# The end of a two-layer Perceiver block on one core: the last groups of the second attention ordered by hand, the residual added by the matmul engine, already turned tokens quantised, stores issued from two engines

## The chip, the cores and the metric

The kernel runs on one core of one Trainium2 chip. The metric is the device time of one execution in microseconds (us). The core has a matmul engine (TensorE, PE in the rows; its weight loads are listed apart as PEld), VectorE (DVE), ScalarE (ACT), GpSimd (POOL) and SyncE (SP), which issues transfers. The engines run their own instruction lists in order and meet only at semaphores. Matmul results land in eight banks of PSUM, each 128 partitions by 512 float32 columns; everything else is in SBUF.

## What is computed

Six residual layers on `x` (4 batches of 128 tokens, 128 channels), each fed with the layer norm of `x`: a strided cross attention over 2048 context rows, a state space layer, a ternary SwiGLU, a gated cross attention, then a self attention with a relative position bias, and an MLP with quantised activations. The change touches the last two:

```
x = x + L1_attn(layernorm(x))        # 16 heads of 8 channels, softmax, out @ w_proj.T + b_proj
x = x + L1_ffn(layernorm(x))

def qlinear(x, W, b):                # L1_ffn is qlinear, gelu, qlinear
    scale = max((max(x) - min(x)) / 255, 1e-8)      # over ALL tokens and channels
    zp    = clip(round(-min(x) / scale) - 128, -128, 127)
    xq    = clip(round(x / scale) + zp, -128, 127)
    return ((xq - zp) @ wq.T) * (scale * w_scale) + b
```

The minimum and maximum run over the whole tensor, so no activation of the MLP can be quantised before the last batch has been normalised, and again not before the last hidden value is there. Rounding is done by adding and taking off `ROUND` = 12582912.

## The kernel before, in words

Each batch `b` is one tile of 128 tokens. `attention(ph)` exists once on PE, DVE and ACT and is run for both attentions (`ph` 0 and 1). In step `t` (0 to 25) the engines work on group `t` of the 16 groups (four heads of one batch each; batch `t // 4`): scores on PE (lines 1242 to 1245), on DVE the bias and row maxima (806), exponentials on ACT (498). Two steps later PE turns the group's probabilities (1264) and DVE copies them out (823). What closes a batch is tied to `t` by a table of numbers on line 63; `due(t, stage)` gives the batch whose stage falls in step `t`:

```
LAG = 2
INVERSE, INVERSE_T, VALUES, SCALE, PROJECT, ADD, RSTD, NORM, TURN = 6, 7, 8, 9, 10, 11, 11, 12, 13
```

The stages of one batch are: reciprocal of the row sums on DVE (850), turned by PE (1281) and copied out (856); the 16 products with the values on PE ("heads", 1293) into bank 5, copied to `o_T` by ACT (511); the inverse sums spread over the channels by PE (1298) into bank 7; their product `attn_T` on DVE (832); the projection on PE into bank 5 (1313); the residual plus bias `xb` added on DVE (838); mean and variance (731, 732); reciprocal deviation by two ACT instructions (430, 431); the normalised tile `xn` (736), and its extremes (784, 785). PE issues the heads of a batch only when the batch before has been added, since both use bank 5 (1289, 1290). For the last two batches the steps 16 to 25 hold little else.

Then the MLP. `extremes(i)` on PE turns the per-partition extremes (1547); DVE folds them to one column (869), puts them on a diagonal (870), PE spreads this to all partitions with a matrix of ones (1550); `range_of_all`, `affine_step` and `affine_bounds` on DVE make scale, its inverse and the clip bounds (873 to 893). DVE scales and rounds `xn` (1087), clips (1091) and takes off `ROUND` into bfloat16 (1095), in two halves; PE turns the four tiles (1556), ACT copies them to `xq_T` (699), and PE makes four hidden chunks (1561), ACT the gelu (703), DVE the extremes of each (1098, 1099). The second quantisation goes the same way, without turning: ACT rounds chunks 0 to 2 (707), DVE rounds chunk 3 (1104), clips all four (1113) and takes off `ROUND` (1121), one clip ahead; PE accumulates four batches over the chunks in the order 0, 3, 1, 2. DVE adds the residual (1127) and SP stores each batch (349), four stores on one queue.

Of the kernel before, what the change touches and what calls it, by code (L numbers as in the profile page):

```python
# [15 lines left out]
ALU = mybir.AluOpType  # L16
ACT = mybir.ActivationFunctionType
F32 = mybir.dt.float32
BF16 = mybir.dt.bfloat16
# [51 lines left out]

BY_PE = tuple(range(3, NS, 2))
# [24 lines left out]
def two_layers(nc, early, cols, late, rows, ctx_T, taps, ctx, out):  # L97
    st = ExitStack()
    with st:
# [164 lines left out]
        ext_diag = sb("ext_diag", [2 * IC, 2, 2 * IC])  # L264
        rng = sb("rng", [P, 2, 2])
        zs = sb("zs", [P, 2, 8])
        t1 = turn("mlp", [NB, D])
        t2 = turn("mlp", [NB, D])
# [17 lines left out]

        def turned_xn(n, b):
# [13 lines left out]
        def turned_xq8(half):  # L301
            return bank[6 + half][:, 0:P].bitcast(BF16)

# [7 lines left out]
            fin ext ext_ps ext_diag rng z_inv z_out xq8 xq8T xq8T_sb hid_ps hid_sb h_round h_q down8""".split()  # L311
# [12 lines left out]
        def _(sp_):  # L324
# [95 lines left out]
        def _(act):  # L420
# [54 lines left out]

            def self_keys(b):
# [6 lines left out]
            def attention(ph):  # L483
                for t in range(NG * (NB - 1) + TURN + 1):
# [21 lines left out]
                    if due(t, VALUES) is not None:  # L506
                        v = ph * NB + due(t, VALUES)
                        act.wait_ge(S["pv"], v + 1)
                        if v >= 1:
                            act.wait_ge(S["attn"], v)  # L510
                        done(act.activation(o_T[:, :], bank[5][:, 0:P], ACT.Copy), "o_sb")
# [25 lines left out]
            done(act.activation(ident_b[:, :], ident, ACT.Copy), "consts")  # L537

# [167 lines left out]
            for c in range(IC - 1):  # L706
                done(act.activation(h_r1[:, c, :], h_T[:, c, :], ACT.Identity, scale=zs[:, 1, 1:2], bias=round_col[:, :]),
                     "h_round")


        @block.vector
        def _(dve):
# [68 lines left out]

            def token_extremes(b):
# [4 lines left out]
            def attention(ph):  # L787
                i_out = 1 if ph == 0 else 5
                for t in range(NG * (NB - 1) + TURN + 1):
# [28 lines left out]
                    if 0 <= t - LAG < 4 * NB:  # L818
                        w = ph * 16 + t - LAG
                        dve.wait_ge(S["probs_T_ps"], w + 1)  # L820
                        if w // NG >= 2:
                            dve.wait_ge(S["pv"], w // NG - 1)
                        done(dve.tensor_copy(probs_T[:, w % (2 * NG)].rearrange("p h k -> p (h k)"),  # L823
                                             bank[3 + w % 2][:, :]), "probs_T_sb")
                    if due(t, SCALE) is not None:

                        v = ph * NB + due(t, SCALE)
                        dve.wait_ge(S["o_sb"], v + 1)
                        dve.wait_ge(S["spread_ps"], v + 1)
                        if v >= 2:  # L830
                            dve.wait_ge(S["proj"], v - 1)
                        done(dve.tensor_tensor(attn_T[:, v % 2, :], o_T[:, :], bank[7][:, P:2 * P], ALU.mult), "attn")
# [12 lines left out]
                    if due(t, INVERSE) is not None:  # L845
                        v = ph * NB + due(t, INVERSE)
                        dve.wait_ge(S["probs"], 4 * v + 4)
                        if v >= 2:
                            dve.wait_ge(S["invT_ps"], v - 1)
                        done(dve.reciprocal(inv_sum[:, v % 2, :], row_sum[:, v % 2, :]), "inv_sum")  # L850
                    if due(t, INVERSE_T) is not None:
                        v = ph * NB + due(t, INVERSE_T)
                        dve.wait_ge(S["invT_ps"], v + 1)
                        if v >= 1:
                            dve.wait_ge(S["spread_ps"], v)
                        done(dve.tensor_copy(inv_T[:, :], bank[7][0:NH, 0:P]), "invT_sb")
# [27 lines left out]
            def affine_bounds(i, w):  # L884
# [3 lines left out]
                at = mark(dve.tensor_scalar(z[:, 7:8], rng[:, i, 1:2], z[:, 1:2], ROUND, ALU.mult, ALU.add))  # L888
# [7 lines left out]
            link(dve.memset(round_col[:, :], ROUND))  # L896
# [757 lines left out]
```

## Time and profile before

| | |
|---|---|
| median of three runs | 275.21 us (273.03 to 277.95) |
| the profiled execution | 274.26 us, span of its records 272.5 us |
| busy over the span | PE 78%, DVE 72%, ACT 60%, POOL 27% |
| granted TensorE clock, mean | 0.906 of 2.4 GHz |
| first instruction of the part touched (copy of the last but one group) | 240.13 us |
| end of the last output store's landing | 272.5 us |

In the rows, a time is the start in us from the span's start, then the duration; `L823` is line 823; `out<-in` are the tiles; in brackets stands the engine's idle time before and who ended it. Tiles that are parts of one large buffer are all called `region`. The 32 us from 240 to the end are where all edits lie.

### The profile page before, as it was taken

The numbers are of one execution on the slowest core, as the hardware profiler recorded it, in microseconds if no ns is written. First come the engines' busy times: TensorE is split into PE (matmuls) and PEld (weight loads), VectorE is DVE, ScalarE is ACT, GpSimd is POOL, SyncE is SP. The second block draws the span as 40 slices with busy tenths as digits, with TensorE's granted clock in tenths as the row PEclk, the third lists the DMA queues.
The fourth block names the chain that finished last, engine by engine and source line by source line (L and its number), as shares of the span: only waits on it lengthen the run. The fifth ranks groups of instructions, "written<-read, shape, count | busy, mean of one in ns | idle before, by whom it ended". The sixth has DMA issues, their size and how long they took to land.

```text
span 272.5 us, 4968 instructions
## 1 busy us (share of the span) xinstructions
PE 211.6 (78%) x1632; PEld 150.0 (55%) x1634; DVE 197.4 (72%) x571; ACT 163.4 (60%) x541; POOL 74.5 (27%) x73
## 2 busy tenths in 40 slices
PE   7797897888996598889908777999987799972313
PEld 4676785777663343444504545877866789851102
DVE  5467668842398599999697665697667599985675
ACT  3685857616882788888077555134536699842520
POOL 6012100099035577878970010000010000001000
PEclk9999999999979799999975799999999799995555
DMA  6999800000005885000000032000000000000001
GB/s 230 432 384 412 357 7 2 1 2 2 0 0 62 93 93 61 2 0 1 0 0 0 4 101 53 0 2 0 2 0 2 0 2 4 1 2 1 0 0 39
DMA packets 6745, 16.06 MB, mean 59 GB/s; under 512 B 320, under 2 KB 5056, under 8 KB 5696
## 3 DMA queue, kind: packets, MB, share of 16 engines
q1 hardware_dynamic: 6720, 15.75, 20.0%
q8 instruction: 13, 0.21, 0.3%
q14 instruction: 12, 0.10, 0.1%
HBM read 13.39 MB, written 2.35 MB: 58 GB/s over the span
## 4 chain that ended last, share of the span: by engine, by line
PE 39%; DVE 27%; ACT 16%; issue 10%; POOL 5%; DMA 1%; DVEq 0%; another core or an unknown queue 0%; ACTq 0%; POOLq 0%
PE bank L1134 33%; POOL region L411 5%; ACT probs L498 4%; DVE region L958 3%; ACT region L600 3%; PE bank L1526 3%; DVE region L806 2%; DVE region L823 2%; ACT region L568 2%; PE bank L1264 2%; DVE region L775 1%; ACT k_groups L446 1%; DVE xn L736 1%; DMA early_sb<-early 1%; DVE stats L731 1%
## 5 line engine op out<-in xcount | busy, mean ns | idle before, releaser
L411 POOL TENSOR_TENSOR region<-region 128x512 f32<-128x512 f32 x32 | 40.3, 1271 | 13.3 <-DVE region L958 8.9
L958 DVE TENSOR_TENSOR_SCAN region<-region,bank 128x512 f32<-128x512 f32 x32 | 38.1, 1210 | 4.8 <-issue 2.0
L1134 PE MATMUL bank<-k_groups,region 128*128 128x128 f32 x256 | 36.1, 287 | 4.1 <-ACT k_groups L446 2.9
L1134 PEld LDWEIGHTS bank<-k_groups,region 128*128 128x128 f32 x256 | 32.2, 198 | 7.0 <-ACT k_groups L446 3.7
L1134 PE MATMUL bank<-region,early_sb 128*128 128x512 f32 x64 | 32.8, 612 | 1.2 <-POOL region L411 1.1
L380 POOL TENSOR_TENSOR xb<-x,rows_sb 128x512 f32<-128x512 f32 x3 | 3.8, 1265 | 102.6 <-DVE x L838 43.3
L498 ACT ACTIVATE probs<-bank,neg_max 128x128 f32<-128x128 f32 x64 | 22.7, 366 | 12.0 <-DVE neg_max L801 11.9
L498 ACT ACTIVATE probs<-region,neg_max 128x128 f32<-128x128 f32 x64 | 24.9, 389 | 5.4 <-DVE neg_max L806 5.2
L430 ACT ACTIVATE lnv<-mv,eps_col 128x1 f32<-128x1 f32 x24 | 7.0, 292 | 32.8 <-DVE mv L732 32.6
L1134 PE MATMUL bank<-ctx_T_sb,region 128*32 128x128 f32 (+1 forms) x288 | 25.0, 312 | 1.9 <-DVE v_heads L743 1.6
L823 DVE COPY region<-bank 128x512 f32<-128x512 f32 x32 | 21.8, 682 | 3.8 <-PE bank L1264 3.8
L1264 PE MATMUL bank<-early_sb,probs 128*128 128x128 f32 x128 | 20.4, 283 | 2.1 <-ACT probs L498 1.5
L600 ACT ACTIVATE region<-region,a_neg 128x508 f32<-128x508 f32 x32 | 21.3, 709 | 0.0
L806 DVE CUSTOM_DVE_ANT_0 region<-bank,region 128x128 f32<-128x128 f32 x64 | 14.5, 282 | 5.4 <-PE bank L1134 5.4
L801 DVE TENSOR_REDUCE neg_max<-bank 128x4 f32<-128x512 f32 x16 | 11.0, 687 | 9.0 <-PE bank L1134 9.0
L1264 PEld LDWEIGHTS bank<-early_sb,probs 128*128 128x128 f32 x128 | 14.8, 144 | 4.2 <-ACT probs L498 2.1
L1134 PEld LDWEIGHTS bank<-region,ctx_sb 128*128 128x128 f32 x128 | 15.4, 192 | 2.9 <-issue 2.9
L1065 DVE COPY region<-bank 128x512 f32<-128x512 f32 x16 | 10.9, 686 | 8.1 <-PE bank L1526 8.1
L686 ACT ACTIVATE region<-bank,shift 128x512 f32<-128x512 f32 x16 | 10.8, 689 | 8.2 <-DVE shift L1042 8.2
L1134 PE MATMUL bank<-region,ctx_sb 128*128 128x128 f32 x128 | 15.6, 275 | 0.0
L1134 PEld LDWEIGHTS bank<-region,early_sb 128*128 128x128 f32 x64 | 11.1, 196 | 7.4 <-POOL region L411 5.0
L1134 PEld LDWEIGHTS bank<-ctx_T_sb,region 128*32 128x32 f32 (+1 forms) x288 | 11.4, 118 | 4.8 <-DVE v_heads L743 1.8
(205 smaller groups left out, 444.6 us busy)
## 6 DMA issues: line engine op xcount, KB each, us to landing
ctx_sb<-ctx SPq DMA_DIRECT2D x4, 1024.0 KB, 25.1
ctx_T_sb<-ctx_T SPq DMA_DIRECT2D x3, 1024.0 KB, 10.1
late_sb<-late SPq DMA_DIRECT2D x1, 2416.0 KB, 19.3
bias_scratch<-bias_vec SPq DMA_DIRECT2D x1, 2040.0 KB, 24.7
ctx_T_sb<-ctx_T SPq DMA_DIRECT2D x2, 512.0 KB, 5.7
region<-bias_scratch SPq DMA_DIRECT2D x1, 1024.0 KB, 5.6
early_sb<-early SPq DMA_DIRECT2D x1, 512.0 KB, 3.6
region<-taps SPq DMA_DIRECT2D x1, 512.0 KB, 20.0
```

The lines of the kernel that those rows point to most:

```text
L411: done(pool.tensor_tensor(read[:, k % 3, :], state[:, k % 3, :], c_sb[:, n % 2, :], ALU.mult), "read")
L498: ins = act.activation(probs[:, w % 4, j, :], src[:, j, :], ACT.Exp, bias=neg_max[:, w % 4, j:j + 1], scale=1.0 if ph == 0 else -1.0, accu ...
L600: done(act.activation(dst, src, ACT.Exp, scale=a_neg[:, hf, n:n + 1]), "decay")
L686: done(act.activation(p2[:, b % 2, g, :], bank[g][:, :], ACT.Exp, bias=shift[:, b:b + 1], accum_out=part_sum[:, b, g:g + 1]), "p2")
L801: done(dve.tensor_reduce(neg_max[:, w % 4, :], src, AX, ALU.max, negate=True), "neg_max")
L806: ins = dve.tensor_tensor_reduce(neg_biased[:, t % 3, j, :], src[:, j, :], rel_bias[:, HG * g + j, :], -1.0, HIGHEST, ALU.add, ALU.min, ne ...
L823: done(dve.tensor_copy(probs_T[:, w % (2 * NG)].rearrange("p h k -> p (h k)"), bank[3 + w % 2][:, :]), "probs_T_sb")
L958: done(dve.tensor_tensor_scan(state[:, k % 3, :], decay[:, k % NDA, :], bank[3 + k % 3][:, :], 0.0, ALU.mult, ALU.add), "state")
L1065: done(dve.tensor_copy(p2_T[:, w % 4].rearrange("p c q -> p (c q)"), bank[4 + w % 2][:, :]), "p2T_sb")
L1134: return pe.matmul(dst, lhsT, rhs, start=start, stop=stop)
L1264: ins = pe.transpose(bank[3 + w % 2][:, j * P:j * P + P], probs[:, w % 4, j, :], ident)
L1526: ins = pe.transpose(bank[4 + w % 2][:, c * P:c * P + P], p2[:, b % 2, g, c * P:c * P + P], ident)
```

## The change

On all three engines the loop of `attention(1)` now ends after step 15, when all groups have been started (`STEPS`), and the rest is written out by hand. In it the last group's turn stands ahead of the spreading of batch 2, the heads of batch 3 wait only for `o_T` of batch 2 and no longer for batch 2's residual, the inverse sums of batch 3 use bank 2, and batches 2 and 3 are projected into banks 0 and 1 on top of a product of the identity and `xb`, which adds the residual in PE. DVE takes moments and `xn` straight from those banks; ACT copies them to `x5` later. PE turns the four `xn` tiles in float32 into bank 6 before the range is known; DVE rounds from that bank, 512 columns at once, and writes `xq_T` itself. The diagonal is replaced by a constant diagonal holding 1/255, with the extremes as broadcast weights. ACT takes `ROUND` off chunk 3. The stores of batches 1 and 3 are issued by ACT.

```diff
+STEPS = NG * (NB - 1) + TURN + 1, 4 * NB
 # sync
-            for b in range(NB):
+            for b in (0, 2):
                 sp_.wait_ge(S["x_ready"], 5 * NB + b + 1)
 # scalar
             attention(1)
+            heads_out(2 * NB - 2)
+            heads_out(2 * NB - 1)
+            rsqrt_var(5, 2)
+            rsqrt_var(5, 3)
             act.preload_act_table_set("gelu_and_others")
-            for b in range(2):
-                act.wait_ge(S["xq8T"], b + 1)
-                done(act.activation(xq_T[:, 2 * b * P:2 * (b + 1) * P], turned_xq8(b), ACT.Copy), "xq8T_sb")
+            for b in (2, 3):
+                act.wait_ge(S["xn"], 5 * NB + b + 1)
+                done(act.activation(X[5][:, b, :], late_proj(b), ACT.Copy), "x_ready")
...
+            act.wait_ge(S["h_clip"], 1)
+            done(act.activation(h_q[:, IC - 1, :], h_r2[:, IC - 1, :], ACT.Identity, bias=neg_round[:, :]), "h_q_last")
+            for b in (1, 3):
+                act.wait_ge(S["x_ready"], 5 * NB + b + 1)
+                act.dma_start(out[b], X[6][:, b, :]).then_inc(S["stored"], 16)
 # vector
-                link(dve.tensor_reduce(ext_row[:, i:i + 1], bank[7][0:2 * IC, 384:512], AX, ALU.max))
-                done(dve.tensor_scalar(ext_diag[:, i, :], ident[0:2 * IC, 0:2 * IC], ext_row[:, i:i + 1], None,
-                                       ALU.mult), "ext_diag")
+                done(dve.tensor_reduce(ext_row[:, i:i + 1], bank[7][0:2 * IC, 384:512], AX, ALU.max), "ext_row")
...
-                link(dve.tensor_scalar(z[:, 6:7], rng[:, i, 0:1], rng[:, i, 1:2], INV255, ALU.add, ALU.mult))
-                link(dve.tensor_scalar(z[:, 0:1], z[:, 6:7], 1e-8, None, ALU.max))
+                link(dve.tensor_scalar(z[:, 0:1], rng[:, i, 0:1], rng[:, i, 1:2], 1e-8, ALU.add, ALU.max))
...
-                link(dve.tensor_scalar(z[:, 2:3], z[:, 7:8], ROUND, ROUND + 255.0, ALU.max, ALU.min))
-                link(dve.tensor_scalar(z[:, 3:4], z[:, 2:3], -1.0, 2.0 * ROUND, ALU.mult, ALU.add))
-                link(dve.tensor_scalar(z[:, 4:5], z[:, 3:4], 255.0, None, ALU.add))
+                link(dve.tensor_scalar(z[:, 2:3], z[:, 7:8], ROUND, ROUND, ALU.add, ALU.max))
+                link(dve.tensor_scalar(z[:, 6:7], z[:, 2:3], ROUND + 255.0, -1.0, ALU.min, ALU.mult))
+                mark(dve.tensor_scalar(z[:, 3:4], z[:, 6:7], 2.0 * ROUND, None, ALU.add))
+                link(dve.tensor_scalar(z[:, 4:5], z[:, 6:7], 2.0 * ROUND, 255.0, ALU.add, ALU.add))
...
+            turned_probs(8 * NB - 2)
+            inverse(2 * NB - 1)
+            normed(5, 1)
+            turned_probs(8 * NB - 1)
+            scaled(2 * NB - 2)
+            inverse_turned(2 * NB - 1)
+            token_extremes(1)
+            scaled(2 * NB - 1)
+            late_moments(2)
+            late_moments(3)
+            late_normed(2)
+            token_extremes(2)
+            late_normed(3)
+            token_extremes(3)
...
+            dve.wait_ge(S["xnT_all"], 1)
+            rounded_at = mark(dve.tensor_scalar(t1, bank[6][:, :], zs[:, 0, 1:2], ROUND, ALU.mult, ALU.add))
             affine_bounds(0, 3)
             after(rounded_at)
+            link(dve.tensor_scalar(t2, t1, zs[:, 0, 3:4], zs[:, 0, 4:5], ALU.max, ALU.min))
+            done(dve.tensor_scalar(xq_T[:, :], t2, -ROUND, None, ALU.add), "xq8")
...
+            first_at = clip(0)
+            clip(last)
+            after(first_at)
+            quantised(0)
+            for c in (1, 2):
+                after(clip(c))
+                quantised(c)
 # tensor
+            def late_project(b):
+                v = NB + b
+                pe.wait_ge(S["xb_ready"], 3)
+                pe.wait_ge(S["neg_max"], 8 * NB)
+                mm(late_proj(b), ident, xb[:, b, :], True, False)
+                pe.wait_ge(S["attn"], v + 1)
+                done(mm(late_proj(b), attn_T[:, v % 2, :], L("w_projT"), False, True), "proj")
...
-            for i, c in enumerate((0, IC - 1, 1, 2)):
+            for i, c in enumerate((0, 1, IC - 1, 2)):
```

The first place is PE from the last three probability turns to the first turned extremes; here before (`inv_T` is the inverse sums, `v_heads` the values, so its row is the heads of one batch, first of batch 2, then of batch 3):

```order
L1264 MATMUL bank3<-early_sb,probs 128x128 x4
L1134 MATMUL bank5<-region,v_heads 32x128 x16
L1134 MATMUL bank7<-inv_T,cols_sb 128x128
L1264 MATMUL bank4<-early_sb,probs 128x128 x4
L1134 MATMUL bank5<-late_sb,attn_T 128x128
L1281 MATMUL bank7<-early_sb,inv_sum 16x128
L1134 MATMUL bank5<-region,v_heads 32x128 x16
L1134 MATMUL bank7<-inv_T,cols_sb 128x128
L1134 MATMUL bank5<-late_sb,attn_T 128x128
L1547 MATMUL bank7<-early_sb,ext 8x128
```

The same place on PE in the changed kernel:

```order
L1183 MATMUL bank5<-region,v_heads 32x128 x16
L1285 MATMUL bank4<-early_sb,probs 128x128 x4
L1183 MATMUL bank7<-inv_T,cols_sb 128x128
L1300 MATMUL bank2<-early_sb,inv_sum 16x128
L1183 MATMUL bank5<-region,v_heads 32x128 x16
L1183 MATMUL bank2<-inv_T,cols_sb 128x128
L1183 MATMUL bank0<-xb,early_sb 128x128
L1183 MATMUL bank0<-late_sb,attn_T 128x128
L1183 MATMUL bank1<-xb,early_sb 128x128
L1183 MATMUL bank1<-late_sb,attn_T 128x128
L1620 MATMUL bank6<-early_sb,xn 128x128 x4
L1626 MATMUL bank7<-early_sb,ext 8x128
```

Both projections have moved behind both heads, and four turns of `xn` stand ahead of the extremes.

The second place is DVE from the first quantisation's rounding to the first gelu extreme; before:

```order
L1087 TENSOR_SCALAR region<-xn,zs 128x512
L888 TENSOR_SCALAR zs<-rng,zs 128x1
L889 TENSOR_TENSOR zs<-zs,w_scale 128x1
L891 TENSOR_SCALAR zs<-zs 128x1
L892 TENSOR_SCALAR zs<-zs 128x1
L893 TENSOR_SCALAR zs<-zs 128x1
L1091 TENSOR_SCALAR region<-region,zs 128x256 x2
L1095 TENSOR_SCALAR xq<-region 128x256 x2
```

And DVE at that place in the changed kernel:

```order
L1137 TENSOR_SCALAR region<-bank6,zs 128x512
L911 TENSOR_SCALAR zs<-rng,zs 128x1
L912 TENSOR_TENSOR zs<-zs,w_scale 128x1
L914 TENSOR_SCALAR zs<-zs 128x1
L915 TENSOR_SCALAR zs<-zs 128x1
L916 TENSOR_SCALAR zs<-zs 128x1
L917 TENSOR_SCALAR zs<-zs 128x1
L1140 TENSOR_SCALAR region<-region,zs 128x512
L1141 TENSOR_SCALAR xq_T<-region 128x512
```

The bounds have one instruction more, the rounding reads a bank, and the last row writes the operand of the hidden matmul; PE's turns and ACT's copies that stood behind it are gone.

## Rows read from the trace of the kernel before

**Rows 1.** The page, part 4: shares of the chain that ended last.
```profile
PE 39%; DVE 27%; ACT 16%; issue 10%; POOL 5%; DMA 1%; DVEq 0%; another core or an unknown queue 0%; ACTq 0%; POOLq 0%
```
**Rows 2.** Windows: length, busy PE, PEld, DVE, ACT, POOL; clock, DMA share, GB/s.
```profile
243.00:245.00 2.00, 1.63 (x37) 1.13 (x34) 1.29 (x5) 0.71 (x3) 0.00 (x0) 1.00 0.04 8
245.00:246.00 1.00, 0.39 (x3) 0.25 (x2) 0.67 (x3) 0.07 (x1) 0.00 (x0) 0.52 0.00 0
262.00:270.00 8.00, 2.84 (x18) 1.96 (x18) 6.36 (x23) 2.22 (x3) 0.00 (x0) 0.50 0.00 1
```
**Rows 3.** Timeline, end of the second attention: start, us, engine, instruction, idle before.
```profile
236.66 1.06 PE L1134 MATMUL bank<-k_groups,region 128*128 128x128 f32 x8
...
240.64 0.48 PE L1134 MATMUL bank<-inv_T,cols_sb 16*128 16x128 f32 x2
...
241.06 0.66 PE L1264 MATMUL bank<-early_sb,probs 128*128 128x128 f32 x4
...
241.75 0.69 DVE L823 COPY region<-bank 128x512 f32<-128x512 f32 x1
242.36 0.28 DVE L832 TENSOR_TENSOR attn_T<-o_T,bank 128x128 f32<-128x128 f32 x1
...
242.69 0.49 PE L1134 MATMUL bank<-late_sb,attn_T 128*128 128x128 f32 x2 [0.98 <-DVE attn_T L832]
...
243.65 1.08 PE L1134 MATMUL bank<-region,v_heads 128*32 128x128 f32 x32 [0.37 <-DVE x L838]
...
245.76 0.80 PE L1134 MATMUL bank<-late_sb,attn_T 128*128 128x128 f32 x2 [0.61 <-DVE attn_T L832]
...
246.92 0.29 DVE L731 BATCH_NORM_STATS2 stats<-x 128x6 f32<-128x128 f32 x1
...
248.02 0.35 DVE L736 TENSOR_SCALAR xn<-x,mv,rstd 128x128 f32<-128x128 f32 x1 [0.60 <-ACT rstd L431]
...
248.94 0.38 PE L1547 MATMUL bank<-early_sb,ext 128*8 128x128 f32 x1 [2.39 <-DVE ext L785]
```
**Rows 4.** Timeline, range and first quantisation.
```profile
249.74 0.22 DVE L870 TENSOR_SCALAR ext_diag<-early_sb,ext_row 8x8 f32<-8x8 f32 x1
250.01 0.59 PE L1134 MATMUL bank<-ext_diag,ones 8*128 8x8 f32 x2 [0.69 <-DVE ext_diag L870]
...
251.08 0.15 DVE L880 TENSOR_SCALAR zs<-zs 128x1 f32<-128x1 f32 x1
251.27 0.16 DVE L881 RECIPROCAL zs<-zs 128x1 f32<-128x1 f32 x1
251.47 0.48 DVE L1087 TENSOR_SCALAR region<-xn,zs 128x512 f32<-128x512 f32 x1
...
252.68 0.74 DVE L1091 TENSOR_SCALAR region<-region,zs 128x256 f32<-128x256 f32 x2
...
254.81 0.13 PEld L1134 LDWEIGHTS bank<-xq_T,wq_w1T 128*128 128x128 bf16 x2 [0.80 <-ACT xq_T L699]
```
**Rows 5.** DVE reading banks, by tile, from 190 us: ns min/median/max, starts.
```profile
L778 DVE TENSOR_SCALAR region<-bank,cols_sb x16: 339/343/351, 202.9 to 223.7; 128x128 f32<-128x128 f32 x16
L823 DVE COPY region<-bank x16: 669/685/692, 209.5 to 241.7; 128x512 f32<-128x512 f32 x16
```
**Rows 6.** Groups by form, 240 to 272.5 us: busy us, mean ns, idle before.
```profile
L1113 DVE TENSOR_SCALAR region<-region,zs 128x512 f32<-128x512 f32 x4 | 2.1, 543 | 0.0
...
L1121 DVE TENSOR_SCALAR region<-region 128x512 bf16<-128x512 f32 x4 | 1.6, 420 | 0.0
```
**Rows 7.** Timeline, second quantisation and output.
```profile
264.90 1.00 DVE L1113 TENSOR_SCALAR region<-region,zs 128x512 f32<-128x512 f32 x2
...
268.73 1.12 DVE L1127 SCALAR_TENSOR_TENSOR x<-bank,zs,xb 128x128 f32<-128x128 f32 x4 [0.57 <-PE bank L1134]
269.11 1.77 SPq L349 DMA_DIRECT2D out<-x  x4
```
**Rows 8.** Transfers by line: count, KB each, median us from issue to landing.
```profile
out<-x SPq DMA_DIRECT2D x4, 64.0 KB, 1.6
```

More of the change, by code:

```diff
@@ L474, in gates, with heads_out @@
                                     ACT.Silu), "gate_sb")
+            def heads_out(v):
+                act.wait_ge(S["pv"], v + 1)
+                if v >= 1:
+                    act.wait_ge(S["attn"], v)
+                done(act.activation(o_T[:, :], bank[5][:, 0:P], ACT.Copy), "o_sb")
             def self_keys(b):
@@ L483, in attention @@
             def attention(ph):
-                for t in range(NG * (NB - 1) + TURN + 1):
+                for t in range(STEPS[ph]):
                     if ph == 0 and t % NG == 3 and t // NG + 1 < NB:
@@ L506, in attention @@
                     if due(t, VALUES) is not None:
[L507 to L511, printed above, removed]
+                        heads_out(ph * NB + due(t, VALUES))
                     if due(t, RSTD) is not None:
@@ L537, in _ @@
             done(act.activation(ident_b[:, :], ident, ACT.Copy), "consts")
+            done(act.activation(ident_255[:, :], ident[0:2 * IC, 0:2 * IC], ACT.Copy, scale=INV255), "consts")
             a_rates = a_neg[:, :, :].rearrange("p a n -> p (a n)")
@@ L788, in attention @@
                 i_out = 1 if ph == 0 else 5
-                for t in range(NG * (NB - 1) + TURN + 1):
+                for t in range(STEPS[ph]):
                     if t < 4 * NB:
@@ L818, in attention @@
                     if 0 <= t - LAG < 4 * NB:
[L819 to L824, printed above, removed]
-                    if due(t, SCALE) is not None:
[L827 to L832, printed above, removed]
+                        turned_probs(ph * 16 + t - LAG)
+                    if due(t, SCALE) is not None:
+                        scaled(ph * NB + due(t, SCALE))
                     if due(t, ADD) is not None:
@@ L845, in attention @@
                     if due(t, INVERSE) is not None:
[L846 to L850, printed above, removed]
-                    if due(t, INVERSE_T) is not None:
[L852 to L856, printed above, removed]
+                        inverse(ph * NB + due(t, INVERSE))
+                    if due(t, INVERSE_T) is not None:
+                        inverse_turned(ph * NB + due(t, INVERSE_T))
                     if ph == 0 and t % NG == 0 and 0 < t // NG < NB:
@@ L1112, in clip, with quantised @@
                     dve.wait_ge(S["h_round"], c + 1)
-                return mark(dve.tensor_scalar(h_r2[:, c, :], h_r1[:, c, :], zs[:, 1, 3:4], zs[:, 1, 4:5],
-                                              ALU.max, ALU.min))
-            order = [0, last, 1, 2]
-            at = clip(order[0])
-            for i in range(IC):
-                following = clip(order[i + 1]) if i + 1 < IC else None
-                after(at)
-                done(dve.tensor_scalar(h_q[:, order[i], :], h_r2[:, order[i], :], -ROUND, None, ALU.add), "h_q")
-                at = following
+                ins = dve.tensor_scalar(h_r2[:, c, :], h_r1[:, c, :], zs[:, 1, 3:4], zs[:, 1, 4:5], ALU.max, ALU.min)
+                return done(ins, "h_clip") if c == last else mark(ins)
+            def quantised(c):
+                done(dve.tensor_scalar(h_q[:, c, :], h_r2[:, c, :], -ROUND, None, ALU.add), "h_q")
+            first_at = clip(0)
[5 more added lines that the diff above has]
+                quantised(c)
             dve.wait_ge(S["xb_ready"], 4)
@@ L1256, in attention @@
                     if 0 <= t - LAG < 4 * NB:
-                        w = ph * 16 + t - LAG
-                        pe.wait_ge(S["probs"], w + 1)
-                        if w >= 2:
-                            pe.wait_ge(S["probs_T_sb"], w - 1)
-                        if w == 1:
-                            pe.wait_ge(S["v_sb"], 1)
-                        for j in range(HG):
-                            ins = pe.transpose(bank[3 + w % 2][:, j * P:j * P + P], probs[:, w % 4, j, :], ident)
-                        done(ins, "probs_T_ps")
+                        turn_probs(ph * 16 + t - LAG)
                     if ph == 0 and t == 2:
@@ L1548, in extremes @@
                      "ext_ps")
-                pe.wait_ge(S["ext_diag"], i + 1)
-                done(mm(bank[7][:, 256:256 + 2 * IC], ones[0:2 * IC, :], ext_diag[:, i, :]), "ext_ps")
-            extremes(0)
-            for h in range(2):
-                pe.wait_ge(S["xq8"], h + 1)
-                for b in range(2):
-                    ins = pe.transpose(turned_xq8(h)[:, b * P:b * P + P], xq[:, 2 * h + b, :], ident_b[:, :])
-                done(ins, "xq8T")
-            pe.wait_ge(S["xq8T_sb"], 2)
+                pe.wait_ge(S["ext_row"], i + 1)
+                done(mm(bank[7][:, 256:256 + 2 * IC], ext_row[:, i:i + 1].to_broadcast([2 * IC, P]), ident_255[:, :]),
+                     "ext_ps")
+            turn_probs(8 * NB - 2)
+            heads(1, 2)
+            turn_probs(8 * NB - 1)
+            spread_inverse(1, 2)
+            turn_inverse(1, 3)
+            heads(1, 3)
+            spread_inverse(1, 3)
+            late_project(2)
+            late_project(3)
+            for b in range(NB):
+                turn_last_xn(b)
+            pe.wait_ge(S["consts"], 3)
+            extremes(0)
+            pe.wait_ge(S["xq8"], 1)
+            pe.wait_ge(S["x_ready"], 5 * NB)
             pe.wait_ge(S["w_quant"], 5)
```

136 lines of the change are left out of this document (94 added, 42 removed).

## Prediction

> **What bounds the kernel now.** I read the page first. No engine is full; in the chain that ended last PE holds 39%, DVE 27% and ACT 16% [rows 1], so the bound moves between engines and a gain must be read from the stage that is edited. All edits lie behind 240 us, so I read the timeline from there, and beside it the waits. The stretch is one chain through DVE, PE and ACT with idle engines around it: from 262 to 270 us PE works 2.84 of 8 us and ACT 2.22, DVE 6.36 [rows 2]. The reader is to see three places where the chain runs through work that need not be on it:
>
> - at the attention's end the heads of batch 3 start at 243.65, 1.90 after DVE began to copy the last turned group at 241.75, since they wait for batch 2's scaling, projection and residual [rows 3];
> - between the clip at 252.68 and the hidden matmul's first weights at 254.81 stand a second clip, two offsets, turns on PE and copies on ACT [rows 4];
> - the four stores are issued one behind the other, 1.77 us in all [rows 7].
>
> Windows give TensorE's clock: full (2.4 GHz) up to 245 us, 0.52 from 245 to 246, half (1.2 GHz) in the last stretch [rows 2].
>
> **The attention's end.** The last group's turn stood behind the spread product; it now takes its place, 240.64 instead of 241.06 [rows 3], so it and DVE's copy come 0.42 earlier: the copy at 241.33. The heads of batch 3 now wait for that copy alone (ACT's copy of batch 2's heads is long done). The copy lasts 0.69 [rows 3]; with 0.1 for the hop the heads start at 242.12, 1.53 earlier than before. Behind them PE issues the spread, both identity products and both projections. The spread starts 1.01 into the heads (they last 1.08 and the next product overlaps their tail [rows 3]) and lasts 0.48, so DVE's product for batch 3 starts at about 243.65.
>
> The identity products are new: each is float32, two passes. Eight passes last 1.06 and two last 0.49 at full clock [rows 3], so a further pass costs 0.095 and four passes 0.68. Batch 2's four start behind the spread's two, at 243.35, and end at 244.05. Batch 3's identity pair fits into the wait for `attn_T` (ready at 243.65 + 0.28 = 243.93), so only its projection counts: 0.49 from 244.0, end 244.5. The additions on DVE (one per batch, about 0.3) are gone. ACT's two copies to `x5` need neither DVE nor PE and have until the hidden matmul, some 4 us later; they stand behind the table load, which the earlier end of ACT's list also moves forward. If that cover were gone they would cost about 0.6.
>
> From moments to `xn` took 1.10 before (246.92 to 248.02) [rows 3]. Reading moments from a bank: the nearest row, a bank read of 128 columns, has 343 ns against 0.35 for `xn` from SBUF [rows 3, 5]; I add nothing, 0.05 each as the other end. Batch 2: moments at 244.10, `xn` at 245.20. DVE then makes `xn` and extremes of batch 2, which take 0.78 from start to next start (0.38 and two of 0.20), so `xn` of batch 3 starts at 245.98. From there to the turned extremes 0.92 as before (248.02 to 248.94) [rows 3]: 246.90. **First term: 248.94 - 246.90 = 2.04 earlier.** Three of PE's four new turns are over by then, the fourth runs while DVE takes the extremes (0.4 free); its cost is nothing, 0.3 if it is late.
>
> **Range, twice.** The diagonal goes, and with it 250.01 - 249.74 = 0.27. One step of the scale goes: 251.27 - 251.08 = 0.19 [rows 4]. The broadcast weights have the same shape as the ones before. Against this, the bounds have one instruction more, issued without a wait: 0.1 (at most a linked step, 0.19). Each range: 0.27 + 0.19 - 0.10 = 0.36; **second term 0.72.**
>
> **Rounding from PSUM.** Before, 512 columns from SBUF took 0.48 [rows 4]; from a bank, 512 float32 columns take 0.685 [rows 5]. DVE's following steps wait for it in order: **third term, 0.20 lost.** The Trainium skill speaks against this edit: "VectorE: DVE Perf Modes", section "Why PSUM operands drop a tier", says a float32 operand in PSUM runs at one element per cycle where an SBUF one can run at two. By the errata section's formulas on that page an estimate is 0.33 us of loss, and the sum would be 0.13 smaller; the rows here show 0.20.
>
> **First quantisation.** Before: 254.81 - 252.68 = 2.13 from clip to weights [rows 4]. Now one clip of 512 columns (0.54), the offset into bfloat16 (0.42) [rows 6], and two hops of 0.04 and 0.05: 1.05. **Fourth term 1.08.** Nothing waits behind it: PE turned `xn` earlier. The gelu, and DVE's eight extremes that pace it, are unchanged.
>
> **Second quantisation.** Before, DVE's list from 264.90: eight instructions, the first addition at 268.73, 3.83 later [rows 7]. Now seven; an offset is started 0.34 and a clip 0.46 before the next. Offset 0, clip 1 and clip 2 go at 0.92, 1.26 and 2.18; the offsets of chunks 1 and 2 must first see their clip end (0.58 each), so chunk 2 is done at 2.76 + 0.42 = 3.18. One hop, one product with its tail (0.38), one hop: addition at 3.65. **Fifth term 0.18**. ACT's offset of chunk 3 takes about 0.7 behind its three roundings, near 1.75, and PE wants it near 2.7: a second of cover; without cover it costs at most the offset DVE gave away, 0.34.
>
> **Stores.** Before, the fourth is issued at 269.11 + 3 x 0.44 = 270.44 [rows 7]. Now each queue issues two, and the fourth waits only for the last addition, done near 269.85: issue 269.90. **Sixth term 0.54**, I take 0.5. ACT issues no transfer in the trace of before. Its bounds: as SP's (0.44 for issue, 1.6 to landing [rows 7, 8]), or an issue without benefit (0).
>
> **Sum.** 2.04 + 0.72 - 0.20 + 1.08 + 0.18 + 0.50 = 4.32 us. Against the profiled execution, 274.26, that gives 269.9; the median of the three runs, 275.21, lies 0.95 above it. I take the median as the level: **270.9 us**. Its own range, from the unknown prices (0.1 for bank reads, 0.3 turn, 0.18 bounds, 0.5 store, 0.6 copies, one way; the rest about 0.5 the other), is 269.9 to 272.3.
>
> **The rivals.**
>
> *The clock falls earlier.* Before, PE is at full clock to 245 us, and the two-pass product takes 0.80 at half clock where it took 0.49 [rows 2, 3]. PE's work is now packed ahead of 244.5, but should the clock fall by 243, a two-pass product costs 0.31 more: the spread and the four products for the projections give at most 1.5, less where one hides in a wait; I take 1.3. Time 270.9 + 1.3 = 272.2. Against it: no longer idle stretch of PE comes before 243 than before. Chance 0.13.
>
> *The reordering gives nothing.* The edits don't do what they say if the end of the attention hangs on DVE rather than on bank 5: DVE has the same two copies, scalings and four groups of extremes and moments, packed. Then the first term shrinks to the two additions and the turn, about 1.0 instead of 2.04, and with the ACT queue giving nothing the time is 270.9 + 1.0 + 0.5 = 272.4. For it: DVE works 0.65 of 243 to 245 already [rows 2]; against: from 241.33 its list sums to 4.2 us (the copy 0.6, five short ones at 0.2, two moments at 0.5, twice 0.78) of the 5.6 until 246.90. Chance 0.14.
>
> *The clock holds to the end.* With denser PE work before 247 it may come back or stay. Each two-pass product in the ranges, each turn of extremes, the hidden and the last products are on the path at half clock; by 0.80 against 0.49 [rows 3] four such places give 1.2. Time 269.7. Chance 0.08: PE works 2.84 of 8 us at half clock later, and didn't recover [rows 2].
>
> *Slower than before: the ACT queue.* Its first transfer is the last thing waited for. At SP a store lands 1.6 after issue [rows 8]. If a store on the new queue needed 1.6 + 4.3 = 5.9 us, the whole gain would be gone; at 7 us the time is 275.21 + 1.1 = 276.3. No row has a small transfer near that. "DMA: Bandwidth & Descriptors" of the Trainium skill, section "Issuing engines are not separate DMA queues", has all queues on the same 16 engines, with only issue time to win; no run yet shows ACT's. Chance 0.04.
>
> **How the numbers follow.** My forecast 0.57, the rivals 0.13, 0.14, 0.08, 0.04, small mixtures 0.04. Faster by over 2% is below 269.7, about what a measurement of this kernel can tell from no change. The forecast lies 1.2 above that, and the three runs spread over 4.9 us, so a good fifth of its chance and half of the third rival's fall there, with some for gains I priced at nothing: 0.22. Slower by over 2% (above 280.7) needs the ACT queue at its worst: 0.02. Within 2%: 0.76. The range takes in the first three rivals and the run-to-run spread of the level: 268.9 to 273.0.
>
> **What would show it.** In the changed profile: PE's heads of batch 3 less than 1 us behind DVE's last copy; the first turned extremes near 246.9; from DVE's row of extremes to the reciprocal 0.46 less, twice; the rounding from the bank at 0.68; 1.05 from clip to hidden weights; the additions near 264.9; the last store issued by ACT within 0.1 of the last addition. The prediction is wrong if PE's clock falls before 244, if the hidden matmul waits for ACT's copies to `x5`, if ACT's offset is late for PE, or if the last store lands more than 2 us after issue.

## The result: 1.1 to 1.6% faster, and the profile after

Over 20 executions of each kernel the changed one has a median of 271.54 us against 274.44: 2.90 us, or 1.1%. The ratio on record is 0.9837, 95% interval 0.981 to 0.9864, which from 274.44 is 4.5 us (3.7 to 5.2), where the sum said 4.32; it uses only the executions within 1.5% of their own kernel's fastest, 18 of 20 before and 13 of 20 after, and of the seven left out after the change one took 1005.69 us and six took 272.89 to 273.23, only just beyond that line. Without the 1005.69 the two means differ by 3.7 us (271.0 and 274.7). So the whole times show a gain of 2.9 to 4.5 us and can't confirm the sum; the tail below can. The median of 271.54 lies 0.6 above the forecast of 270.9, inside the range of 268.9 to 273.0.

The profiled execution of the changed kernel took 272.99 us, only 1.27 less than that of before. The traces show why the two totals hide the gain. Take as the *tail* the stretch from DVE's copy of the last but one group to the end of the span. It starts at 240.13 before and at 243.26 here, with only two small new instructions ahead of it; from there on the tail is 32.34 us before and 27.94 after, 4.40 less. (The profile prints a span to 0.1 us; the tails here use the spans to 0.01 us that the traces hold, 272.47 and 271.20. The expectations below use the printed ones and can be off by 0.05.) The timeline of the changed kernel at the attention's end (start, us, engine, instruction, idle before), to be held against [rows 3]:

```profile
243.26 0.67 DVE L804 COPY region<-bank 128x512 f32<-128x512 f32 x1
...
243.77 0.65 PE L1285 MATMUL bank<-early_sb,probs 128*128 128x128 f32 x4
...
244.46 0.69 DVE L804 COPY region<-bank 128x512 f32<-128x512 f32 x1 [0.17 <-PE bank L1285]
...
245.21 1.08 PE L1183 MATMUL bank<-region,v_heads 128*32 128x128 f32 x32 [0.16 <-DVE region L804]
...
246.63 0.49 PE L1183 MATMUL bank<-xb,early_sb 128*128 128x128 f32 x2
...
246.95 0.39 PE L1183 MATMUL bank<-late_sb,attn_T 128*128 128x128 f32 x2
...
247.38 0.30 DVE L1112 BATCH_NORM_STATS2 stats<-bank 128x6 f32<-128x128 f32 x1 [0.30 <-PE bank L1183]
...
248.49 0.41 DVE L1117 TENSOR_SCALAR xn<-bank,mv,rstd 128x128 f32<-128x128 f32 x1 [0.15 <-ACT rstd L437]
...
249.33 0.40 DVE L1117 TENSOR_SCALAR xn<-bank,mv,rstd 128x128 f32<-128x128 f32 x1
...
250.22 0.45 ACT L712 ACTIVATE x<-bank 128x128 f32<-128x128 f32 x2
250.37 0.08 PEld L1626 LDWEIGHTS bank<-early_sb,ext 128*8 128x8 f32 x1 [0.44 <-issue]
```

The heads of batch 3 (245.21) now start 0.75 behind the last copy (244.46), where it was 1.90. The MLP, against [rows 4]:

```profile
251.04 0.38 PE L1183 MATMUL bank<-ident,ext_row 8*128 8x8 f32 x2 [0.37 <-DVE ext_row L895]
...
252.11 0.75 DVE L1137 TENSOR_SCALAR region<-bank,zs 128x512 f32<-128x512 f32 x1
...
253.64 0.55 DVE L1140 TENSOR_SCALAR region<-region,zs 128x512 f32<-128x512 f32 x1
254.22 0.43 DVE L1141 TENSOR_SCALAR xq_T<-region 128x512 bf16<-128x512 f32 x1
254.70 0.13 PEld L1183 LDWEIGHTS bank<-xq_T,wq_w1T 128*128 128x128 bf16 x2 [3.37 <-DVE xq_T L1141]
```

From clip to weights it is one clip and one offset. The end, against [rows 7]; the second queue is ACT's:

```profile
264.41 1.00 DVE L1159 TENSOR_SCALAR region<-region,zs 128x512 f32<-128x512 f32 x2
...
265.44 0.72 ACT L723 ACTIVATE region<-region,neg_round 128x512 bf16<-128x512 f32 x1
...
268.06 1.12 DVE L1176 SCALAR_TENSOR_TENSOR x<-bank,zs,xb 128x128 f32<-128x128 f32 x4 [0.48 <-PE bank L1183]
268.44 0.85 SPq L355 DMA_DIRECT2D out<-x  x2
268.70 0.88 ACTq L726 DMA_DIRECT2D out<-x  x2
```

And the windows (length, busy PE, PEld, DVE, ACT, POOL, then the granted clock), against [rows 2]: full clock holds until almost 253 here, where before it was gone at 245.1.

```profile
246.00:252.00 6.00, 3.31 (x29) 2.10 (x20) 3.62 (x15) 2.92 (x8) 1.20 (x1) 1.00 0.00 0
252.00:253.00 1.00, 0.00 (x0) 0.00 (x0) 0.96 (x4) 0.00 (x0) 0.07 (x1) 0.96 0.00 0
253.00:254.00 1.00, 0.00 (x0) 0.00 (x0) 0.90 (x6) 0.00 (x0) 0.00 (x0) 0.50 0.00 0
```

Stage by stage, from starts in the two timelines (us):

| stage, start to start | before | after | won | forecast |
|---|---|---|---|---|
| last but one copy to turned extremes | 8.81 | 7.11 | 1.70 | 2.04 |
| to the first rounding | 2.53 | 1.74 | 0.79 | 0.46 |
| rounding to clip | 1.21 | 1.53 | -0.32 | -0.30 |
| clip to hidden weights | 2.13 | 1.06 | 1.07 | 1.08 |
| weights to second extremes | 6.41 | 6.41 | 0 | 0 |
| to the second rounding | 2.47 | 2.03 | 0.44 | 0.46 |
| rounding to clip | 1.21 | 1.27 | -0.06 | -0.10 |
| clip to first addition | 3.83 | 3.65 | 0.18 | 0.18 |
| addition to the end | 3.74 | 3.14 | 0.60 | 0.50 |
| sum | 32.34 | 27.94 | 4.40 | 4.32 |

### The profile page after: what moved, and what is told of

Same layout as the page of the kernel before. It is cut to its first block, busy times and chain, and to the rows that moved or that the text cites. A ratio compares the mean times of both kernels' runs of the same rounds, so it can differ in the third digit from the quotient of the medians.

```text
span 271.2 us, 4973 instructions
## 1 busy us (share of the span) xinstructions
PE 213.4 (79%) x1636; PEld 151.8 (56%) x1638; DVE 195.7 (72%) x565; ACT 164.1 (61%) x543; POOL 74.5 (27%) x73
## 4 chain that ended last, share of the span: by engine, by line
PE 41%; DVE 26%; ACT 15%; issue 10%; POOL 4%; another core or an unknown queue 2%; DMA 1%; DVEq 0%; ACTq 0%; POOLq 0%
PE bank L1183 34%; POOL region L417 4%; ACT probs L510 4%; DVE region L983 3%; PE bank L1589 3%; DVE region L850 2%; DVE region L804 2%; ACT region L609 2%; ACT region L577 2%; PE bank L1285 2%; DVE region L793 1%; DMA early_sb<-early 1%; ACT k_groups L452 1%; ACT region L593 1%
## 5 line engine op out<-in xcount | busy, mean ns | idle before, releaser
L1183 PE MATMUL bank<-region,early_sb 128*128 128x512 f32 x64 | 31.9, 598 | 1.3 <-POOL region L417 1.1
L1183 PE MATMUL bank<-ctx_T_sb,region 128*32 128x128 f32 (+1 forms) x288 | 28.1, 349 | 1.9 <-DVE v_heads L761 1.6
L1183 PEld LDWEIGHTS bank<-ctx_T_sb,region 128*32 128x32 f32 (+1 forms) x288 | 13.0, 133 | 5.7 <-issue 2.4
```

Source lines behind the costliest of these rows:

```text
L1183: return pe.matmul(dst, lhsT, rhs, start=start, stop=stop)
```

## Experiments

There are twelve runs, two of them of the unedited kernels. In the two traces that each of those has, the tail repeats within 0.02 us (32.34 and 32.35; 27.94 and 27.92), and so does every mark inside it, so that edits worth tenths are read here from single traces, while whole times of one kernel spread over some five us. Five runs are a single execution: `b0` 274.90 us, `x1` 270.40, `x2` 271.81, `x5` 269.03, `x9` 274.83. Marks below, as `+7.10`, are us from the start of the tail.

**The same kernels once more.** No edit.

> The changed kernel once more, unedited. The tail is the stretch from the start of DVE's copy of the last but one group's turned probabilities to the end of the span: 32.37 us before (272.50 - 240.13), 27.94 after (271.20 - 243.26). Theory A (the gain is the edited tail, step by step, and what lies ahead of it only varies from execution to execution): tail 27.9 within 0.3, whatever time lies ahead of it. Theory B (the changed kernel also slows what lies ahead, since its copy started 3.13 us later than before): the copy again starts at 243 or later.

Measured: tail 27.92, starting at 240.44; 270.15 us in all. Ratio over four executions 0.9825 (0.979 to 0.986). Theory A holds, B is out: what lies ahead of the tail does vary by itself.

> The kernel before once more, unedited, for where TensorE's clock falls. In the first trace of before it fell at 245.2 us, so the last projection took 0.80 and the first range was made at half clock; in the changed kernel it fell near 253. Theory A (where the clock falls varies from execution to execution, and the first trace of before had it early by about 0.5 us of cost): tail 31.9 if it falls behind the first range, 32.4 if not. Theory B (the denser attention end of the changed kernel keeps the clock up): it falls near 245 again, tail 32.4.

Measured: tail 32.35, 274.9 us. The clock falls between 245 and 246 again, as theory B has it; `x4` below shows that the order is not all of it:

```profile
245.00:246.00 1.00, 0.79 (x17) 0.40 (x6) 0.68 (x3) 0.50 (x3) 0.00 (x0) 0.85 0.06 16
246.00:247.00 1.00, 0.60 (x2) 0.50 (x2) 0.35 (x2) 0.00 (x0) 0.00 (x0) 0.50 0.00 0
```

**The attention's end undone.** Both loops run 26 steps again, the hand-written tails, `late_project`, the late moments and ACT's copies go, bank 7 holds all inverse sums.

```diff
-STEPS = NG * (NB - 1) + TURN + 1, 4 * NB
+STEPS = (NG * (NB - 1) + TURN + 1,) * 2
```

> The changed kernel with the attention's end as before (26 steps from the table, residual added by DVE from bank 5, inverse sums in bank 7), everything behind it as changed. Theory A: the tail grows by the attention term, 1.7 us by the two traces (8.81 against 7.11 from the copy to the turned extremes), and by 0.3 more where the clock is at half level again when the first range is made: tail 29.6 to 30.0. Rival (reordering gives nothing, the gain is in the quantisation): tail within 0.5 of 27.9.

Measured: tail 29.44, ratio 0.9894 (0.985 to 0.994), 0.16 short of theory A's 29.6 to 30.0 and far from the rival. Turned extremes at +8.56 against +7.11 and +8.81 before. The reordering is real and worth 1.45 where the clock is full in both, 0.07 more up to the first inverse; theory A had booked the whole 1.70 for it. What the comparison with before adds is clock: this kernel kept it full to the first range, and its projection of batch 3 took 0.49 where [rows 3] has 0.80, its turned extremes 0.27 where it was 0.38:

```profile
248.89 0.49 PE L1163 MATMUL bank<-late_sb,attn_T 128*128 128x128 f32 x2 [0.61 <-DVE attn_T L805]
...
251.85 0.27 PE L1602 MATMUL bank<-early_sb,ext 128*8 128x128 f32 x1 [0.28 <-DVE ext L822]
```

PE's list up to the first of these rows is that of before, where twice the clock had already fallen. So the order alone does not set the place of the fall; this tail started at 243.26, as did the first changed execution's, and in both the clock fell at +9.7. Among tails that start between 239.6 and 240.8, it fell at +4.9 in both traces of before and at +8.0 to +8.3 in the changed order (`a0`, `x1`, `x3`, `x5`, `x10`, `x12`). There the denser order goes with a later fall; two traces of the old order are few to call it the cause.

**Residual back on DVE.** `late_project` makes one product, DVE adds `xb` and takes moments and `xn` from `x5`; ACT copies nothing.

```diff
-                mm(late_proj(b), ident, xb[:, b, :], True, False)
...
+                done(dve.tensor_tensor(X[5][:, b, :], late_proj(b), xb[:, b, :], ALU.add), "x_ready")
```

> The changed kernel with the residual of the last two batches added by DVE to x5 (no identity products, moments and xn from SBUF, no copies on ACT). Theory A: DVE pays 0.33 for batch 2's addition on the chain (proj to moments); the bank reads of moments and xn and the identity pair give back about 0.2 (0.06 for each xn, 0.19 for one pair that is not needed): tail 27.96 plus 0.1 to 0.5. Rival (the identity products sit in PE's idle time and the addition is the whole price): plus 0.66.

Measured: tail 28.82, 0.89 longer, more than either theory said. The turned extremes came at +7.81, 0.71 late, and one row stands out. DVE's `xn` of batch 2 took 1.02 instead of 0.34, and ended 0.07 behind GpSimd's addition of the output bias:

```profile
246.26 1.26 POOL L386 TENSOR_TENSOR xb<-x,rows_sb 128x512 f32<-128x512 f32 x1 [41.43 <-DVE x L1110]
...
246.57 1.02 DVE L1117 TENSOR_SCALAR xn<-x,mv,rstd 128x128 f32<-128x128 f32 x1
...
248.03 0.34 DVE L1117 TENSOR_SCALAR xn<-x,mv,rstd 128x128 f32<-128x128 f32 x1
```

Another 0.21 is the range's product at half clock (0.59 for 0.38), since the clock fell at 249.6 in this execution.

**GpSimd's addition moved.** To tell that collision from the price of adding on DVE, GpSimd's last addition was held back, first to the first scale:

```diff
+                    if i == 5:
+                        pool.wait_ge(S["z_out"], 1)
```

> The kernel x2 (residual of the last two batches added by DVE), with GpSimd's addition of the output bias held back until the first scale is there. In x2 the tail was 28.81, and DVE's first late xn took 1.02 instead of 0.34 while GpSimd's addition (1.26) ran. Theory P (GpSimd's addition, released by DVE's last residual, holds DVE's SBUF to SBUF xn up; the change avoids that since ACT's late copies release it): xn back at 0.35, tail 28.81 - 0.68 = 28.1 or 27.9, depending on where the clock falls. Rival (the 0.68 is the price of the additions and of reading x5): tail 28.8.

Measured: turned extremes at +7.10, exactly as in the changed kernel, but the weights at +12.00 and the tail 28.49. The collision had moved to the clip, 1.12 instead of 0.55:

```profile
254.50 1.26 POOL L388 TENSOR_TENSOR xb<-x,rows_sb 128x512 f32<-128x512 f32 x1 [46.30 <-DVE zs L911]
...
254.92 1.12 DVE L1142 TENSOR_SCALAR region<-region,zs 128x512 f32<-128x512 f32 x1
```

Then to the first gelu chunk (`hid_sb` in place of `z_out`):

> x9 with GpSimd's addition held back further, to the first gelu chunk, where DVE only reduces. In x9 the turned extremes came at +7.10 as in the changed kernel, but GpSimd's addition now ran beside DVE's clip and the hidden weights came at +12.00 instead of +11.44. Theory P (GpSimd's addition holds up whichever SBUF to SBUF scaling of 128 or more columns DVE wants, and DVE's two residual additions cost nothing against PE's identity products): turned extremes +7.10, weights +11.44, tail 27.9. Rival (reading x5 and adding on DVE costs something that x9 hid): tail 28.2 or more, with the difference ahead of the weights.

Measured: +7.10, +11.44, tail 27.94 (the changed kernel: 27.94 and 27.92); the ratio over four executions is 0.9885 with an interval from 0.978 to 0.999 that says no more than that.

```profile
245.57 0.32 DVE L1119 TENSOR_SCALAR xn<-x,mv,rstd 128x128 f32<-128x128 f32 x1
...
250.56 0.55 DVE L1142 TENSOR_SCALAR region<-region,zs 128x512 f32<-128x512 f32 x1
...
253.27 1.26 POOL L388 TENSOR_TENSOR xb<-x,rows_sb 128x512 f32<-128x512 f32 x1 [49.51 <-ACT region L715]
```

So the residual through PE is worth nothing by itself: with it on DVE the first moments start at +4.23 instead of +4.12, and each `xn` from SBUF gives 0.06 to 0.09 back. What the edit does is to release GpSimd by ACT's late copies instead of by DVE's addition, and so to put GpSimd's 1.26 us beside DVE instructions that read banks or single columns. The Trainium skill, "SBUF — State Buffer", section "SBUF: two separate sides", says that VectorE and GpSimd share a port pair as an exclusive lock: whichever starts first keeps it for the whole instruction, against a VectorE instruction in a two-port mode. These three runs agree that DVE's scaling waits: 0.68 and 0.57 us of stretch, and none where GpSimd ran beside reductions. They don't bear out the whole instruction: both stretched scalings ended as if they had begun 0.27 before the end of GpSimd's record. The kernel before shows the same 0.27. There too GpSimd's addition, released by DVE's last residual, runs beside this stretch, but `xn` starts late enough and takes its usual 0.35:

```profile
247.03 1.26 POOL L380 TENSOR_TENSOR xb<-x,rows_sb 128x512 f32<-128x512 f32 x1 [43.26 <-DVE x L838]
```

That ends at 248.29, and `xn` began at 248.02 [rows 3]. In the new order `xn` comes sooner behind the last residual, and with the residual on DVE the two meet. (The ends of GpSimd's records are rough, so the 0.27 may be one of the record and not of the engine.)

**First quantisation as before.**

```diff
-            link(dve.tensor_scalar(t2, t1, zs[:, 0, 3:4], zs[:, 0, 4:5], ALU.max, ALU.min))
-            done(dve.tensor_scalar(xq_T[:, :], t2, -ROUND, None, ALU.add), "xq8")
+            clipped_at = [mark(dve.tensor_scalar(t2[:, h], t1[:, h], zs[:, 0, 3:4], zs[:, 0, 4:5],
+                                                 ALU.max, ALU.min)) for h in halves]
...
+                    ins = pe.transpose(turned_xq8(h)[:, b * P:b * P + P], xq[:, 2 * h + b, :], ident_b[:, :])
```

> The changed kernel with the first quantisation as before: round xn from SBUF, clip and offset in halves, turn in bfloat16 on PE, copy on ACT. Theory A: the rounding gets 0.27 shorter and the stretch from clip to the hidden matmul's weights 1.07 longer: tail 0.8 longer, 28.7. Rival (turning in float32 before the range only moves PE's work in front of the extremes): tail within 0.3 of 27.9, since the turned extremes would come that much earlier.

Measured: tail 28.74, 0.81 longer; extremes at +7.11 and first inverse at +8.65 as in the changed kernel, weights at +12.25 against +11.44. Ratio 0.9891 (0.983 to 0.996). Theory A; PE's float32 turns cost nothing in front of the extremes.

```profile
249.41 0.49 DVE L1142 TENSOR_SCALAR region<-xn,zs 128x512 f32<-128x512 f32 x1
250.68 0.73 DVE L1146 TENSOR_SCALAR region<-region,zs 128x256 f32<-128x256 f32 x2
...
252.81 0.13 PEld L1193 LDWEIGHTS bank<-xq_T,wq_w1T 128*128 128x128 bf16 x2 [0.80 <-ACT xq_T L718]
```

**One queue.** SP issues all four stores, ACT none.

> The changed kernel with all four stores on SP. Theory A (what is won is issue time): from the first addition to the end of the span 3.77 us as before instead of 3.14, tail 28.5. Rival (all stores run on the same engines, the landing of the last one decides): 3.2 us, tail 28.0.

Measured: tail 28.53, 0.60 longer, all of it behind the first addition (3.73 for 3.13). Issue time is what the second queue saves; ACT's stores land 1.6 us after issue like SP's.

```profile
264.88 1.12 DVE L1173 SCALAR_TENSOR_TENSOR x<-bank,zs,xb 128x128 f32<-128x128 f32 x4 [0.48 <-PE bank L1180]
265.25 1.77 SPq L355 DMA_DIRECT2D out<-x  x4
```

**Rounding from SBUF.** ACT copies the four turned tiles, and DVE rounds the copy.

```diff
+            done(act.activation(xnT_sb, bank[6][:, :], ACT.Copy), "xnT_copied")
...
-            rounded_at = mark(dve.tensor_scalar(t1, bank[6][:, :], zs[:, 0, 1:2], ROUND, ALU.mult, ALU.add))
+            rounded_at = mark(dve.tensor_scalar(t1, xnT_sb, zs[:, 0, 1:2], ROUND, ALU.mult, ALU.add))
```

> The changed kernel, but ACT copies the turned xn out of the bank (0.69) before the range is there, and DVE rounds from SBUF. Theory A (the price of rounding from the bank is 0.27, 0.75 against 0.485 in the traces): tail 27.96 - 0.27 = 27.7. Rival (ACT's copy comes late, behind the table load and two copies, near 251.4 where DVE wants it at 249.3 + or the bank is held when DVE reads another): tail 27.9 or more.

Measured: tail 27.66, 0.27 shorter, all of it up to the weights (+11.18 against +11.44). ACT's copy ends 1.0 before the rounding.

```profile
246.87 0.60 ACT L715 ACTIVATE region<-bank 128x512 f32<-128x512 f32 x1
...
248.43 0.49 DVE L1140 TENSOR_SCALAR region<-region,zs 128x512 f32<-128x512 f32 x1
```

**PE filled in its idle time.** `keep_warm(n, 4)` issues `n` unread products.

```diff
             extremes(0)
+            keep_warm(20, 4)
...
+            keep_warm(30, 4)
             extremes(1)
+            keep_warm(20, 4)
```

> The changed kernel with products nobody reads (bfloat16, 256 columns, into bank 4) in PE's idle stretches of the MLP: 20 behind the first range, 30 behind the hidden products, 20 behind the second range. Theory A (half clock costs in the MLP: 0.2 at the first hidden product, 0.32 in the second range, 0.15 or more at the last products): clock 1.0 to the end, tail 27.96 - 0.7 = 27.3. Rival (the fills run at half clock at first and stand in the way): tail 28 to 30.

Measured: tail 27.82, 0.11 shorter, ratio 0.9891 (0.985 to 0.993), as a whole no better than the change's 0.9837. Both theories have a share. The 20 ran at half clock and held the hidden product up, weights at +11.84 for +11.44; behind it the clock was full, and the second range took 1.51 for 1.82:

```profile
250.81 4.02 PE L1183 MATMUL bank<-ones 128*128 128x256 bf16 x20
...
254.66 1.03 PE L1183 MATMUL bank<-xq_T,wq_w1T 128*128 128x512 bf16 x4
```

**Together.** `x5`, and DVE's clips of chunks 1 and 2 one behind the other, PE taking the chunks as 0, 3, 1, 2.

```diff
-            for c in (1, 2):
-                after(clip(c))
+            clipped_at = [clip(c) for c in (1, 2)]
+            for c, at in zip((1, 2), clipped_at):
+                after(at)
                 quantised(c)
```

> The changed kernel with x5 (rounding from SBUF, tail 27.62) and with DVE's clips of chunks 1 and 2 issued one behind the other before their offsets (PE takes the chunks as 0, 3, 1, 2). Theory A (two waits of 0.12 on DVE go, and the product behind the last chunk hides behind them): tail 27.4. Rival (PE's products of chunk 1 come later and fill what DVE gives): 27.6. Against the kernel before: 274.5 - 4.95 = 269.5, ratio 0.982.

Measured: tail 27.50, ratio 0.9865 (0.981 to 0.992). Clip to first addition is 3.49 for 3.65, and the same 0.16 is left at the end: most of the 0.2 of theory A, but not all; PE, at half clock, still has chunk 1's products in front of the last chunk's, as the rival has it.

> x10 with unread products in PE's idle time, fewer than in x6: 12, 26 and 16. In x6 the first 20 ran at half clock and held the hidden matmul up by 0.40, while full clock gave back 0.13, 0.31 and 0.06 behind it. Theory A: without the hold-up the tail is 27.4 - 0.5 = 26.9, ratio to before 0.980. Rival (with fewer fills the clock does not come back before the second range): tail 27.4.

Measured: tail 27.05, 0.88 shorter than the changed kernel's; the weights at +11.20 are no longer held up, and the clock is full again from just behind the start of the hidden products to the second turned extremes. It then fell, so the last 16 ran at half clock, 3.42 us; they ended as the first chunk was ready. The ratio is 0.9873 (0.983 to 0.992).

```profile
250.81 2.74 PE L1187 MATMUL bank<-ones 128*128 128x256 bf16 x12
...
260.19 0.27 PE L1630 MATMUL bank<-early_sb,ext 128*8 128x128 f32 x1 [2.31 <-DVE ext L1148]
```

By its tail this is the shortest version. Its whole times don't show it faster than the change: its ratio of 0.9873 is not lower, and what lies ahead of the tail varies by more than the 0.88. That it beats the change in time is not shown.

## Why the prediction was right

The sum and its stages hold in the tail, 4.40 where 4.32 was said, but two of its errors cancel, and so do two in the whole time.

- **The attention's end** was the right place and worth 1.70 where 2.04 was said. Its first half holds to the hundredth: copy 0.42 earlier, heads of batch 3 1.57 earlier (1.53 said), `attn_T` at +3.53 (3.52). The 0.34 went on small things: the projection's four passes 0.15 later than counted, `xn` from a bank 0.41 each where I took 0.35 (0.06 twice, where the other end I had kept was 0.05 each), and 0.07 more for the hop from DVE's last extreme to PE (0.12 for 0.05). `x3` has the same 0.12 without PE's turns in front, so they are not its cause; what is stays open. Of the 1.70, `x4` puts 0.25 down to clock. The term took the projection at full clock without pricing it: in both traces of before that product lies behind the fall and takes 0.3 more.
- **The step on the residual** was wrong in its reason. The text booked DVE's two additions as won. `x12` shows that they cost no more than what replaces them, and `x2` that keeping them on DVE costs 0.68 for another reason: they release GpSimd's addition next to DVE's scaling. The prediction never asked what that last addition releases. That the changed kernel escapes the collision is luck.
- **The ranges** won 0.46 less 0.02 where the clock was alike (0.44, the second) and 0.79 where it was not: products of 0.38 and 0.59 took 0.27 and 0.38. This is the rival "the clock holds" at its first two places; it did not hold to the end (half clock from 253), and so the rival's 1.2 was not there. The surplus of 0.33 made up for the first term's loss: the closeness of the sum is in part luck. With the 0.25 above, nearly 0.6 of the 4.40 is clock and not work taken off the chain.
- **Rounding from the bank** cost 0.27 (0.75 against 0.48), where the copy's row said 0.20; with the bounds 0.32 for 0.30. `x5` takes 0.26 of it back. The estimate by the formulas of the Trainium skill, "VectorE: DVE Perf Modes", errata section, was 0.33; the measured loss lies between the two.
- **First quantisation** 1.07 for 1.08, confirmed by `x3`: 0.81 between the same two marks, where 1.07 less 0.27 was due.
- **Second quantisation** 0.18 for 0.18; ACT's offset ended at 266.16, a us before PE got to it at 267.1.
- **Stores** 0.60 for 0.50, and `x1` gives the same 0.60. ACT's stores landed as fast as SP's, 1.6 us after issue; the slower rival has nothing left.
- "The clock falls earlier" and "the reordering gives nothing" are out by the windows and by `x4`. None of the signs named for being wrong came: the clock fell at 252.9, ACT's copies to `x5` ended at 250.67, four us before the hidden weights, and its offset was in time.
- **The level.** I set the sum against the median of three, 275.21, and spread the range by the variation of whole times. The median of 20 is 274.44, 0.77 lower; the medians differ by 2.90 where the sum has 4.32. The level was too high and the gain in whole times smaller than the sum, and that the forecast lies within 0.6 of the median is luck to that extent. Over the 14 profiled executions at hand the tail starts between 239.58 and 240.77 in the eight whose clock was full over the first 24 us, and between 241.19 and 244.55 in the six where it dipped there. Ahead of it only two small instructions are new (a constant on DVE, an 8x8 copy on ACT), and single times of before spread as widely; that the dip is the cause is what the windows suggest, and no run tests it. Nor is it known whether the changed kernel meets the dip more often: neither of the two traces of before has it, and six of the twelve others do.

## What to carry to other kernels

Read an edit at the end of a program from a stretch with a fixed start, and compare start to start: here two traces of one kernel gave the same tail within 0.02 us, where twenty whole times leave 1.5 us of interval. Before crediting an edit with work taken off an engine, see what that engine's last instruction releases: the gain of moving the residual was only that GpSimd's addition did not run beside DVE's scalings. Do on operands whose range is not known yet all that commutes with the scale, such as the turn, and leave only elementwise steps behind it.

## What the runs showed of the hardware

- One GpSimd addition of 128x512 float32 (1.26 us) stretched a DVE scaling of 128 columns from 0.34 to 1.02 and one of 512 columns from 0.55 to 1.12, both SBUF to SBUF. It left reductions of 512 columns at 0.68 (`x12`) and steps on one column at 0.15 (`x9`). Both stretched scalings ended as if begun 0.27 before the end of GpSimd's record.
- Two float32 passes of a product took 0.49 at full and 0.80 at half clock (`x4`, [rows 3]); in the ranges 0.38 and 0.59.
- Unread products begun at half clock are themselves slow (20 of 256 columns: 4.02 us, against 2.36 for 20 at full clock in the same execution, `x6`) and can delay what they are to speed up; 12 in that gap held nothing up (`x11`).
- A store of 64 KB issued by ACT landed 1.6 us after issue, as one issued by SP did.
